# Attention stage: query and key loads of 8 KB rows, 8 in place of 12, three units ahead

## The chip, the cores and the metric

The kernel runs on one core of a Trainium2 chip. The time is device microseconds (us) of one execution: lower is better. Beside the plain runs there is one profiled execution, from which all rows come. Its clock is the granted clock of TensorE: 1.00 stands for 2.4 GHz, 0.50 for 1.2 GHz.

## The reference, cut to what matters

A two-layer gated block works on x of shape (8, 256, 512). Four stages follow one another: an attention with a mask, a ternary-weight feed-forward layer, a long convolution, and an fp8 feed-forward layer. The change touches the attention and the projections ahead of it:

```
q = Wq @ layernorm(x) + bq;  k = Wk @ ctx + bk;  v = Wv @ ctx + bv      # (8, 256, 512)
q, k, v -> (8, 16 heads, 16, 512)                                      # channel = 16 * head + d
dot = einsum('bhdt,bhds->bhts', q, k) / 4
dot = mask * dot - (1 - mask) * 1e6;  amap = softmax(dot) * mask
out = einsum('bhts,bhds->bhdt', amap, v);  x = x + tanh(g) * out
```

## The kernel before, in words

The projection stage (`phase_project`) computes q and k in f32 and splits each into three bf16 parts whose sum is the value. They go to HBM tensors `q_parts` and `k_parts` of shape (8 batches, 3 parts, 256 channels, 512 positions).

The attention stage (`phase_attention`) works on 16 units; a unit u is half a batch, that is 8 heads. For a unit, the SBUF tiles `q_stack` and `k_stack` (`Q` and `K` in the code) hold six blocks of 16 partitions each. A block is one bf16 part of the 16 channels of a head, the 8 heads side by side in the free dimension. With `Q_PART = (0, 0, 1, 1, 0, 2)` and `K_PART = (0, 1, 0, 1, 2, 0)` one bf16 matmul over 128 partitions sums the part products that make an f32 product. Rows 96 to 127 hold the masks and the row maxima. Both tiles have four slots; unit u uses slot u % 4.

Per unit:

- TensorE makes 32 tiles of scores for the maxima (`max_tile`, L707), which VectorE reduces (`reduce_tile`, L793), then the same scores transposed (L728), which ScalarE turns into exponentials (L675), then the products with V (L738). The maxima of unit u+2's first half and of unit u+1's second half are made during unit u. The first tile of unit u+2 comes at step k = 4 of 8 and waits for the loads of that unit, `qk_loaded`.
- The maxima are turned (L716), copied to `mrow` (L653) and sent by DMA into `q_stack` (`place_max`, L529). The first scores of a unit wait for it (`m_placed`).
- `gather_den` (L544 to L550) sends the sums of exponentials of unit u-1 to HBM, waits until they are there (`den_out`), and reads them back spread over 128 partitions. VectorE takes their reciprocal (`invert`, L807); in VectorE's order it stands behind the four tiles of step k = 4. Then come `store_inv` (L556), `spread_inv` (L562) and GpSimd's multiplications (L623 to L631).

All DMAs are issued by SyncE, in program order, on one queue. For each unit u the order is: loads of unit u+2 (`load_unit`, 12 of 128 KB and two of mask rows), `gather_den` of u-1, in every second unit V and mask, `store_inv`, `place_max` of u+1, `spread_inv`, one weight load of 768 KB (L524, wait for `w_ternary`). The load of unit u+2 needs the slot of unit u-2, and so waits for `scores_done` of that unit. The stage begins with the loads of units 0 and 1 (`fresh`: the masks go in once the rows are zeroed), the V load, and two weight loads.

Of the kernel before, what the change touches and what calls it, by code (L numbers as in the profile page):

```python
# [11 lines left out]
P = 128  # L12
B = 8
C = 256
L = 512
CT = C // P
LT = L // P
ROWT = B * CT
HEADS, HD = 16, 16
UH = 8  # L20
# [5 lines left out]
Q_PART = (0, 0, 1, 1, 0, 2)  # L26
K_PART = (0, 1, 0, 1, 2, 0)
BLOCKS = len(Q_PART)
MASK_ROW = BLOCKS * HD
MAX_ROW = MASK_ROW + BLOCKS  # L30
EXTRA = BLOCKS + 2


def batch_loads(b, par):
# [3 lines left out]

def slot_loads(b, par):

    return (2 * BLOCKS + 2) * (8 * (b - par) + 16)


class Core:
# [384 lines left out]
def phase_attention(core, ctx, A):  # L429
# [8 lines left out]
    with ExitStack() as free:  # L438
# [6 lines left out]
        Q = sb("q_stack", [P, 4, UH, L], BF16)  # L445
        K = sb("k_stack", [P, 4, UH, L], BF16)
# [32 lines left out]
        HALF = TILES // 2  # L479
        STATS_STEP, DEN_STEP, TURN_STEP = 2, 4, 4  # L480
        TURN_SLOT = EACH * (TURN_STEP + 1)
        LOADS = 16 * (2 * BLOCKS + 2)

        def tiles(k, more, more2):

# [7 lines left out]
        def over_batches(eng, batch):  # L493

            batch(0, 0, True, False)
            with eng.Fori(0, (B - 2) // 2) as i:
                batch(2 * i + 1, 1, False, False)
                batch(2 * i + 2, 0, False, False)
            batch(B - 1, 1, False, True)

        with nc.Block() as block:

            @block.sync
            def _(sp):
                def load_unit(b, slot, h, fresh=False):
                    for blk in range(BLOCKS):
                        for dst, src, part in ((Q, core.q_parts, Q_PART[blk]), (K, core.k_parts, K_PART[blk])):
                            s = src[bass.ds(b, 1), part, h * P:(h + 1) * P, :]
                            sp.dma_start(dst[blk * HD:(blk + 1) * HD, slot],
                                         s.rearrange("a (h d) l -> d (a h) l", d=HD)).then_inc(qk_loaded[slot], 16)  # L510
                    if fresh:
                        sp.wait_ge(zeroed[slot], 2)
                    for dst, src in ((Q, core.mask_q), (K, core.mask_k)):
                        s = src[bass.ds(b, 1)].rearrange("a r l -> r a l").to_broadcast([EXTRA, UH, L])
                        sp.dma_start(dst[MASK_ROW:MASK_ROW + EXTRA, slot], s).then_inc(qk_loaded[slot], 16)

                def load_batch(b, par):
                    sp.dma_start(V[:, par].rearrange("p a h d -> p (a h d)"),
                                 core.v_rows[bass.ds(b, 1)].rearrange("a p n -> p (a n)")).then_inc(v_loaded[par], 16)
                    sp.dma_start(mb[:, par, :], A["mask"][bass.ds(b, 1), 0, :].to_broadcast([P, L]))\  # L520
                        .then_inc(v_loaded[par], 16)

                def load_weights(u, h):
                    sp.dma_start(wc[:, h], A["w3"][bass.ds(u, 1)].rearrange("a p m l -> p (a m) l"))\  # L524
                        .then_inc(wc_loaded[h], 16)

                def place_max(v, slot, h):
                    sp.wait_ge(mrow_ready, v + 1)
                    sp.dma_start(Q[MAX_ROW:MAX_ROW + 2, slot], mrow[:]).then_inc(m_placed[h], 16)  # L529

                load_unit(0, 0, 0, fresh=True)
                load_unit(0, 1, 1, fresh=True)
                load_batch(0, 0)
                load_weights(0, 0)
                load_weights(1, 1)
                sp.wait_ge(zeroed[2], 2)
                sp.wait_ge(zeroed[3], 2)
                place_max(0, 0, 0)

                def gather_den(u, h, b):  # L540

                    sp.wait_ge(u_ready, 2 * u + 2)
                    rows = core.den_rows[h].rearrange("(g two) l -> two g l", two=2)
                    sp.dma_start(rows[0], num[HD:P:32, h, :]).then_inc(den_out[h], 16)  # L544
                    sp.dma_start(rows[1], odd[HD:P:32, h, :]).then_inc(den_out[h], 16)
                    sp.wait_ge(den_out[h], 32 * (b + 1))
                    sp.dma_start(den[:, h, :], core.den_rows[h].rearrange("q (s n) -> (q s) n", n=DW))\
                        .then_inc(den_placed[h], 16)
                    for g in range(4):
                        sp.dma_start(num[32 * g + HD:32 * g + 32, h, :], odd[32 * g:32 * g + HD, h, :])\  # L550
                            .then_inc(num_placed[h], 16)

                def store_inv(u, h):

                    sp.wait_ge(inv_ready, u + 1)
                    sp.dma_start(core.inv_rows[h].rearrange("q (s n) -> (q s) n", n=DW), inv[:, h, :])\  # L556
                        .then_inc(inv_out[h], 16)

                def spread_inv(h, b):

                    sp.wait_ge(inv_out[h], 16 * (b + 1))
                    sp.dma_start(inv_all[:, h, :], core.inv_rows[h].unsqueeze(1).to_broadcast([UH, HD, L]))\  # L562
                        .then_inc(all_placed[h], 16)

                def batch(b, par, first, last):
                    for h in range(2):
                        u = 2 * b + h
                        if not last:
                            if not first:
                                sp.wait_ge(scores_done, 2 * STEPS * (u - 1))  # L570
                            load_unit(b + 1, 2 * (1 - par) + h, h)
                        if not (first and h == 0):
                            gather_den(u - 1, 1 - h, b + h - 1)
                        if h == 1 and not last:
                            if not first:
                                sp.wait_ge(pv_step, 2 * STEPS * b)
                                sp.wait_ge(w_ready, 2 * b)
                            load_batch(b + 1, 1 - par)
                        if not (first and h == 0):
                            store_inv(u - 1, 1 - h)  # L580
                        if h == 0:
                            place_max(u + 1, 2 * par + 1, 1)
                        elif not last:
                            place_max(u + 1, 2 * (1 - par), 0)
                        if not (first and h == 0):
                            spread_inv(1 - h, b + h - 1)
                        if not (first and h == 0) and not (last and h):
                            sp.wait_ge(w_ternary, 3 * u)
                            load_weights(u + 1, 1 - h)
                    if last:  # L590
                        gather_den(u, h, b)
                        store_inv(u, h)
                        spread_inv(h, b)

                over_batches(sp, batch)

            @block.gpsimd
            def _(pool):
# [1230 lines left out]
```

## Time and profile before

| | us |
|---|---|
| median of 3 runs | 1375.86 (1374.11 to 1379.04) |
| profiled execution, its own time | 1371.15 |
| its span | 1369.3 |
| TensorE busy | 1113.3 (81%) |
| VectorE busy | 1033.2 (75%) |
| ScalarE busy | 668.1 (49%) |
| GpSimd busy | 523.4 (38%) |

The span is the time between the first and the last instruction of the profile. The attention stage lies from about 159 us to 645 us. Idle time in a row is followed by what ended it. The DMA share is the mean busy share of the 16 DMA engines; packets that overlap on an engine can carry it over 1.

### The profile page before, as it was taken

The page shows a single profiled execution, that of the slowest core. Times are in us where ns is not written, and L with a number is a line of the kernel's source. Part 1 is how long each engine was busy: PE and PEld are TensorE (multiplying, and loading weights), DVE is VectorE, ACT ScalarE, POOL GpSimd, SP SyncE. Part 2 cuts the span into 40 slices and gives each one's busy share as a digit, 9 for nine tenths or more (in the row PEclk, how much of TensorE's full clock was granted, in tenths as well). Part 3 has the DMA queues.
Part 4 walks back from the last instruction along what each step waited for, and adds up shares of the span by engine and source line. Part 5 has one row for each costly group of instructions (what it writes and reads, how often), then busy time and mean ns, then how long its engine had stood idle before and what let it go on. Part 6 is the DMA issues. An engine that isn't in the chain of part 4 may idle for free. (4 is left out here: it accounts for less than half of the span.)

```text
span 1369.3 us, 16346 instructions
## 1 busy us (share of the span) xinstructions
PE 1113.3 (81%) x4725; PEld 447.5 (33%) x4802; DVE 1033.2 (75%) x1587; ACT 668.1 (49%) x783; POOL 523.4 (38%) x384
## 2 busy tenths in 40 slices
PE   0887279998879987983799998599999999259777
PEld 0443112222222222220344444344444444134232
DVE  5765488887767877751799997388788887767898
ACT  0355308776657766684466665211000000386796
POOL 0466601244332442355011111477888787000021
PEclk9999659999989999997999999799999999579889
DMA  7398797677756776621311110111111111000011
GB/s 266 127 338 319 199 146 83 119 153 108 125 90 124 151 111 115 114 71 58 151 47 46 40 36 16 35 62 62 62 62 50 58 62 46 1 0 0 0 62 62
DMA packets 84274, 129.33 MB, mean 94 GB/s; under 512 B 13544, under 2 KB 53864, under 8 KB 83696
## 3 DMA queue, kind: packets, MB, share of 16 engines
q1 hardware_dynamic: 84224, 128.72, 38.8%
q8 instruction: 24, 0.39, 0.1%
q14 instruction: 26, 0.21, 0.1%
HBM read 104.44 MB, written 21.89 MB: 92 GB/s over the span
## 5 line engine op out<-in xcount | busy, mean ns | idle before, releaser
L793 DVE TENSOR_REDUCE mneg<-ps_m 128x1 f32<-128x512 f32 x512 | 322.2, 683 | 93.8 <-PE ps_m L707 78.3
L1337 PE MATMUL ps_y<-kv,toeplitz_sb 128*128 128x512 f32 x640 | 279.6, 596 | 8.7 <-POOL kv L1249 8.7
L675 ACT ACTIVATE probs<-ps_s 128x1024 f32<-128x1024 f32 x256 | 249.9, 1022 | 51.9 <-PE ps_s L728 51.9
L707 PE MATMUL ps_m<-k_stack,q_stack 128*128 128x512 bf16 x489 | 181.9, 410 | 55.3 <-DMA k_stack<-mask_k 50.4
L1337 PEld LDWEIGHTS ps_y<-kv,toeplitz_sb 128*128 128x128 f32 x640 | 121.1, 191 | 155.0 <-issue 155.0
L728 PE MATMUL ps_s<-q_stack,k_stack 128*128 128x512 bf16 x492 | 151.0, 387 | 21.1 <-ACT probs L675 11.2
L738 PE MATMUL ps_o<-probs,v_all 128*17 128x512 f32 x1024 | 140.1, 620 | 0.4 <-ACT probs L675 0.4
L1249 POOL TENSOR_TENSOR kv<-vT,ctxT_sb 128x2048 f32<-128x2048 f32 x32 | 118.7, 3711 | 40.0 <-PE ps_y L1337 32.6
L972 PE MATMUL ps_g<-w,xT_f 128*128 128x512 bf16 x491 | 116.7, 384 | 8.4 <-DVE h_f L1119 6.6
L623 POOL TENSOR_TENSOR inv_all<-inv_all,mb_b 128x512 f32<-128x512 f32 x16 | 20.4, 1274 | 254.9 <-DMA inv_all<-inv_rows 254.9
L707 PEld LDWEIGHTS ps_m<-k_stack,q_stack 128*128 128x128 bf16 x512 | 42.2, 99 | 219.4 <-DVE mneg L793 104.5
L1403 DVE TENSOR_TENSOR z<-ps_y,ctxT_sb 128x1024 f32<-128x1024 f32 x64 | 77.9, 1218 | 47.3 <-PE ps_y L1337 47.3
L1302 ACT ACTIVATE w_anchor<-w_f 128x512 f32<-128x512 f32 x32 | 20.1, 628 | 180.6 <-DMA w_f<-in_w 180.6
L1154 POOL TENSOR_TENSOR X<-X,down_sums 128x512 f32 (+1 forms) x16 | 20.5, 1283 | 195.6 <-ACT down_sums L1015 195.6
L1660 PE MATMUL ps_fp<-w 128*128 128x512 bf16 x251 | 67.7, 423 | 21.5 <-DVE w L1727 10.9
L1411 DVE TENSOR_REDUCE vT<-z 128x256 f32<-128x2304 f32 x32 | 81.7, 2553 | 1.1
L54 DVE BATCH_NORM_STATS2 bn<-X (+1 forms) x64 | 42.3, 682 | 42.8 <-POOL X L631 21.2
L728 PEld LDWEIGHTS ps_s<-q_stack,k_stack 128*128 128x128 bf16 x512 | 45.8, 98 | 81.0 <-ACT probs L675 33.9
L641 POOL TENSOR_SCALAR w<-w_sweep 128x512 bf16<-128x512 f32 x48 | 70.4, 1488 | 1.3
L1027 ACT ACTIVATE sg_f<-ps_g,sc_f 128x512 f32<-128x512 f32 x64 | 42.7, 686 | 57.0 <-PE ps_g L972 37.7
L972 PEld LDWEIGHTS ps_g<-w,xT_f 128*128 128x128 bf16 x512 | 48.4, 99 | 65.1 <-DVE h_f L1119 10.3
L326 PE MATMUL ps_a<-xn_a,w_qkv 128*128 128x512 f32 x64 | 30.6, 622 | 38.4 <-DVE xn_a L365 38.4
(163 smaller groups left out, 1662.6 us busy)
## 6 DMA issues: line engine op xcount, KB each, us to landing
w_sweep<-in_w SPq DMA_DIRECT2D x8, 1536.0 KB, 8.5
q_stack<-q_parts SPq DMA_DIRECT2D x96, 128.0 KB
k_stack<-k_parts SPq DMA_DIRECT2D x96, 128.0 KB
w_sweep<-in_w SPq DMA_DIRECT2D x16, 768.0 KB, 6.5
w_sweep<-in_w SPq DMA_DIRECT2D x16, 512.0 KB, 3.3
toeplitz_sb<-in_toeplitz SPq DMA_DIRECT2D x32, 256.0 KB, 2.6
w_f<-in_w SPq DMA_DIRECT2D x32, 256.0 KB, 2.9
q_parts<-qk_part SPq DMA_DIRECT2D x24, 256.0 KB, 4.0
```

The source lines that it names most:

```text
L641: nc.gpsimd.tensor_scalar(core.w3[:, m].rearrange("p a b -> p (a b)")[:, u * L:(u + 1) * L], wc[:, h, m, :], MAGIC, None, ALU.subtract).th ...
L675: nc.scalar.activation(pr[:, k % 2, 2 * slot:2 * slot + 2, :], S[:, 2 * slot:2 * slot + 2, :], ACT.Exp).then_inc(exp_done, 1)
L707: nc.tensor.matmul(M[:, bank(j), :], Q[:, slot, hd, tc * P:(tc + 1) * P], K[:, slot, hd, :], start=True, stop=True).then_inc(max_mm, 1)
L728: mm = nc.tensor.matmul(S[:, g, :], K[:, slot4, hd, (k % LT) * P:(k % LT + 1) * P], Q[:, slot4, hd, :], start=True, stop=True)
L738: mm = nc.tensor.matmul(O[32 * g:32 * g + HD + 1, :], V[:, par, sc, h * UH + 2 * g + G, :], pr[:, k % 2, g, :], start=(sc == 0), stop=(sc ...
L793: nc.vector.tensor_reduce(mneg[:, h, tile % LT, tile // LT:tile // LT + 1], M[:, bank(j), :], AX.X, ALU.max, negate=True).then_inc(max_red, 1)
L972: mm = nc.tensor.matmul(G[:, c % 2, j, :], xT[:, par, k, :], wt[:, k, c * L:(c + 1) * L], start=(k == 0), stop=(k == LT - 1))
L1249: nc.gpsimd.tensor_tensor(kv[:, g % 2].rearrange("p l (b j i) -> p (l b) j i", b=B, j=GROUP), over_j(group(vT, g)), over_i(group(cT, g)), ...
L1337: mm = nc.tensor.matmul(Y[:, q % 3, l2, :], T[:, g % 2, (lt - m) * P:(lt - m + 1) * P], kv[:, g % 2, m, :], start=(m == 0), stop=(m == lt))
L1403: nc.vector.tensor_tensor(z[:, g % 2, NB // 2 * half:NB // 2 * (half + 1), :, 0:GROUP], Y[:, q % 3].rearrange("p l (b j i) -> p (l b) j i" ...
L1411: nc.vector.tensor_reduce(group(vT, g), z[:, g % 2], AX.X, ALU.add).then_inc(red_ready, 1)
L1660: mm = nc.tensor.matmul(D[:, r, :], h8[:, j % 4, L * t + r * P:L * t + (r + 1) * P], proj[:, ot, :], start=(i == 0 and t == 0), stop=(i == ...
```

## The change

Four things change together.

1. The columns of Wq and Wk and the biases are permuted on the host (`by_dim`), in each group of 128 channels from (head, d) to (d, head). In `q_parts` and `k_parts` the 8 heads of one d then follow one another: a row of a block is one piece of 8 x 512 x 2 = 8192 bytes, where it was 8 pieces of 1024 bytes.
2. A unit is loaded by 8 DMAs and not 12. Four of them fill 32 partitions (256 KB): for q, the same part twice (a source with a step of 0 over 2 outside the 16 rows); for k, parts 0 and 1 (a source with 2 parts outside the 16 rows). Four fill 16 partitions (128 KB). The destination and the bytes are as before. `LOADS` follows with 10 in place of 14.
3. The loads of unit u+3, not u+2, are issued in unit u. They wait for `scores_done` of unit u-1. Unit 2's loads come ahead of the loop, and before the weight loads.
4. SyncE's program is written out over all batches, in place of a loop.

The core of the diff:

```diff
-    return (2 * BLOCKS + 2) * (8 * (b - par) + 16)
+    return QK_LOADS * (8 * (b - par) + 16)
...
-                    for blk in range(BLOCKS):
-                        for dst, src, part in ((Q, core.q_parts, Q_PART[blk]), (K, core.k_parts, K_PART[blk])):
-                            s = src[bass.ds(b, 1), part, h * P:(h + 1) * P, :]
-                            sp.dma_start(dst[blk * HD:(blk + 1) * HD, slot],
-                                         s.rearrange("a (h d) l -> d (a h) l", d=HD)).then_inc(qk_loaded[slot], 16)
+                    for dst, src, row, part, times in ((Q, core.q_parts, 0, 0, 2), (K, core.k_parts, 0, None, 1),
+                                                       (Q, core.q_parts, 2, 1, 2), (K, core.k_parts, 2, None, 1),
+                                                       (Q, core.q_parts, 4, 0, 1), (K, core.k_parts, 4, 2, 1),
+                                                       (Q, core.q_parts, 5, 2, 1), (K, core.k_parts, 5, 0, 1)):
+                        if part is None:
+                            s = src[b, 0:2, h * P:(h + 1) * P, :].rearrange("j (d h) l -> j d (h l)", d=HD)
+                            rows = 2
+                        else:
+                            s = src[b, part, h * P:(h + 1) * P, :].rearrange("(d h) l -> d (h l)", d=HD)
+                            s = s.unsqueeze(0).to_broadcast([times, HD, UH * L])
+                            rows = times
+                        sp.dma_start(dst[row * HD:(row + rows) * HD, slot].rearrange("p h l -> p (h l)"), s)\
+                            .then_inc(qk_loaded[slot], 16)
...
                 load_batch(0, 0)
+                load_unit(1, 2, 0, fresh=True)
                 load_weights(0, 0)
                 load_weights(1, 1)
-                sp.wait_ge(zeroed[2], 2)
-                sp.wait_ge(zeroed[3], 2)
                 place_max(0, 0, 0)
...
-                        if not last:
-                            if not first:
-                                sp.wait_ge(scores_done, 2 * STEPS * (u - 1))
-                            load_unit(b + 1, 2 * (1 - par) + h, h)
+                        if u + 3 < 2 * B:
+                            if u:
+                                sp.wait_ge(scores_done, 2 * STEPS * u)
+                            load_unit((u + 3) // 2, (u + 3) % 4, 1 - h, fresh=u == 0)
...
+        return np.ascontiguousarray(v.reshape(v.shape[:-1] + (CT, P // HD, HD)).swapaxes(-1, -2).reshape(v.shape))
...
-        "wqT": np.ascontiguousarray(inputs["L0_xattn_Wq"].T), "wkT": np.ascontiguousarray(inputs["L0_xattn_Wk"].T),
+        "wqT": by_dim(inputs["L0_xattn_Wq"].T), "wkT": by_dim(inputs["L0_xattn_Wk"].T),
```

On SyncE, the end of what is issued ahead of the loop, in the kernel before. L509 is one of the twelve loads of unit 1, L515 the masks, L518 and L520 V and its mask, L524 the weights, L529 the maxima of unit 0.

```order
L509 DMA k_stack<-k_parts 16x8x512
L515 DMA q_stack<-mask_q 8x8x512 [waits zeroed1]
L515 DMA k_stack<-mask_k 8x8x512
L518 DMA v_all<-v_rows 128x1088
L520 DMA mb_b<-in_mask 128x512
L524 DMA w_sweep<-in_w 128x1536 x2
L529 DMA q_stack<-mrow 2x8x512 [waits mrow_ready,zeroed3,zeroed2]
```

The same place now (L527 is V, L518 the loads of unit 2, L524 its masks, L533 the weights, L538 the maxima):

```order
L527 DMA v_all<-v_rows 128x1088
L529 DMA mb_b<-in_mask 128x512
L518 DMA q_stack<-q_parts 32x1x4096
L518 DMA k_stack<-k_parts 32x1x4096
...
L518 DMA q_stack<-q_parts 16x4096
L518 DMA k_stack<-k_parts 16x4096
L524 DMA q_stack<-mask_q 8x8x512 [waits zeroed2]
L524 DMA k_stack<-mask_k 8x8x512
L533 DMA w_sweep<-in_w 128x1536 x2
L538 DMA q_stack<-mrow 2x8x512 [waits mrow_ready]
```

Unit 2's ten DMAs, which stood behind the maxima of unit 0, now stand ahead of them.

On SyncE, unit 1 of the loop in the kernel before, from the last load to the weights:

```order
L509 DMA k_stack<-k_parts 16x8x512
L515 DMA q_stack<-mask_q 8x8x512
L515 DMA k_stack<-mask_k 8x8x512
L544 DMA den_rows<-num 4x512 [waits u_ready]
L545 DMA den_rows<-odd_heads 4x512
L547 DMA den<-den_rows 128x32 [waits den_out0]
L550 DMA num<-odd_heads 16x512 x4
L518 DMA v_all<-v_rows 128x1088
L520 DMA mb_b<-in_mask 128x512
L556 DMA inv_rows<-inv 128x32 [waits inv_ready]
L529 DMA q_stack<-mrow 2x8x512 [waits mrow_ready]
```

The same unit now, where the loads are those of unit 4:

```order
L518 DMA q_stack<-q_parts 32x1x4096 [waits scores_done]
L518 DMA k_stack<-k_parts 32x1x4096
...
L524 DMA q_stack<-mask_q 8x8x512
L524 DMA k_stack<-mask_k 8x8x512
L552 DMA den_rows<-num 4x512 [waits u_ready]
L553 DMA den_rows<-odd_heads 4x512
L555 DMA den<-den_rows 128x32 [waits den_out0]
L558 DMA num<-odd_heads 16x512 x4
L527 DMA v_all<-v_rows 128x1088
L529 DMA mb_b<-in_mask 128x512
L564 DMA inv_rows<-inv 128x32 [waits inv_ready]
L538 DMA q_stack<-mrow 2x8x512 [waits mrow_ready]
```

The order within a unit is the same: the sums of exponentials still go out behind the unit's loads. What moved is that the first load has a wait for `scores_done`, here of unit 0, and that it fills 32 partitions. The orders of the other engines are unchanged.

## Rows read from the trace of the kernel before

**Rows 1.** Waits from 140 to 600 us: total us, times, longest.

```profile
PE ps_m L707 <- DMA k_stack<-mask_k: 50.4, 11, 22.2
...
PE ps_s L728 <- DMA k_stack<-mask_k: 8.0, 3, 3.6
```

**Rows 2.** Timeline, ScalarE: copies that end a unit (start us, us).

```profile
230.57 0.60 ACT L664 ACTIVATE odd_heads<-ps_o 128x512 f32<-128x512 f32 x1 [0.85 <-PE ps_o L738]
...
254.42 0.60 ACT L664 ACTIVATE odd_heads<-ps_o 128x512 f32<-128x512 f32 x1 [0.85 <-PE ps_o L738]
...
305.44 0.60 ACT L664 ACTIVATE odd_heads<-ps_o 128x512 f32<-128x512 f32 x1 [0.77 <-PE ps_o L738]
...
336.02 0.60 ACT L664 ACTIVATE odd_heads<-ps_o 128x512 f32<-128x512 f32 x1 [0.86 <-PE ps_o L738]
...
561.71 0.60 ACT L664 ACTIVATE odd_heads<-ps_o 128x512 f32<-128x512 f32 x1 [0.85 <-PE ps_o L738]
```

**Rows 3.** Timeline, SyncE's issues, one unit of the loop.

```profile
301.65 0.33 SPq L509 DMA_DIRECT2D q_stack<-q_parts  x1
...
309.27 0.50 SPq L545 DMA_DIRECT2D den_rows<-odd_heads  x1
320.06 0.36 SPq L547 DMA_DIRECT2D den<-den_rows  x1
...
327.13 0.70 SPq L529 DMA_DIRECT2D q_stack<-mrow  x1
...
330.16 0.34 SPq L509 DMA_DIRECT2D q_stack<-q_parts  x1
```

**Rows 4.** SyncE's own waits, whole span.

```profile
SPq L547 <- DMA den_rows<-odd_heads: 138.9, 16, 12.4
```

**Rows 5.** Busy time by stretch: per engine; clock, DMA share, GB/s.

```profile
311.00:313.00 2.00, 1.95 (x14) 0.70 (x8) 1.67 (x4) 1.82 (x3) 2.00 (x2) 1.00 1.13 136
...
317.00:319.00 2.00, 0.00 (x0) 0.00 (x0) 0.00 (x0) 0.00 (x0) 0.00 (x0) 0.79 0.37 55
...
321.00:323.00 2.00, 2.00 (x10) 0.16 (x8) 0.85 (x2) 0.00 (x0) 0.00 (x0) 0.50 0.21 44
```

**Rows 6.** Busy time by stretch: V, maxima, reciprocals, ctxT, each alone.

```profile
579.50:581.00 1.50, 1.50 (x11) 0.25 (x10) 1.10 (x2) 1.50 (x3) 0.00 (x0) 1.00 1.00 395
605.00:605.50 0.50, 0.50 (x6) 0.13 (x8) 0.00 (x0) 0.50 (x2) 0.00 (x0) 1.00 0.11 33
...
639.50:640.00 0.50, 0.00 (x0) 0.00 (x0) 0.00 (x0) 0.00 (x0) 0.00 (x0) 0.50 0.51 197
648.00:656.00 8.00, 4.02 (x13) 1.57 (x14) 3.01 (x10) 0.60 (x1) 0.00 (x0) 0.50 1.01 425
```

**Rows 7.** Timeline, SyncE, last unit, nothing else on the queue.

```profile
631.09 0.50 SPq L545 DMA_DIRECT2D den_rows<-odd_heads  x1
632.78 0.32 SPq L547 DMA_DIRECT2D den<-den_rows  x1
```

**Rows 8.** VectorE's reciprocals, the whole run: min, median, max ns.

```profile
L807 DVE RECIPROCAL inv<-den x16: 341/344/353, 244.0 to 634.4; 128x32 f32<-128x32 f32 x16
```

**Rows 9.** Timeline, VectorE, step 4 of unit 5.

```profile
325.33 0.34 DVE L807 RECIPROCAL inv<-den 128x32 f32<-128x32 f32 x1
```

**Rows 10.** Timeline, TensorE: last scores of unit 4.

```profile
300.76 0.59 PE L728 MATMUL ps_s<-q_stack,k_stack 128*128 128x512 bf16 x2
```

**Rows 11.** Timeline, SyncE: first load; maxima of unit 0.

```profile
158.97 0.36 SPq L509 DMA_DIRECT2D q_stack<-q_parts  x1
...
199.14 0.81 SPq L529 DMA_DIRECT2D q_stack<-mrow  x1
```

**Rows 12.** Timeline, TensorE: first maxima, first scores.

```profile
176.38 1.06 PE L707 MATMUL ps_m<-k_stack,q_stack 128*128 128x512 bf16 x2 [22.20 <-DMA k_stack<-mask_k]
...
204.75 0.59 PE L728 MATMUL ps_s<-q_stack,k_stack 128*128 128x512 bf16 x2
```

**Rows 13.** Timeline, VectorE: last statistics of the attention stage.

```profile
645.08 0.69 DVE L54 BATCH_NORM_STATS2 bn<-X 128x6 f32<-128x512 f32 x1 [9.81 <-POOL X L631]
```

More of the change, by code:

```diff
@@ L31 @@
 EXTRA = BLOCKS + 2
+QK_LOADS = 10
 def batch_loads(b, par):
@@ L481, in phase_attention @@
         TURN_SLOT = EACH * (TURN_STEP + 1)
-        LOADS = 16 * (2 * BLOCKS + 2)
+        LOADS = 16 * QK_LOADS
         def tiles(k, more, more2):
@@ L513, in load_unit @@
                     for dst, src in ((Q, core.mask_q), (K, core.mask_k)):
-                        s = src[bass.ds(b, 1)].rearrange("a r l -> r a l").to_broadcast([EXTRA, UH, L])
+                        s = src[b].unsqueeze(1).to_broadcast([EXTRA, UH, L])
                         sp.dma_start(dst[MASK_ROW:MASK_ROW + EXTRA, slot], s).then_inc(qk_loaded[slot], 16)
@@ L593, in batch @@
                         spread_inv(h, b)
-                over_batches(sp, batch)
+                for b in range(B):
+                    batch(b, b % 2, b == 0, b == B - 1)
             @block.gpsimd
@@ L1803, in chunks, with by_dim @@
         return np.ascontiguousarray(np.stack(w, axis=2).transpose(1, 0, 2, 3))
+    def by_dim(v):
+        return np.ascontiguousarray(v.reshape(v.shape[:-1] + (CT, P // HD, HD)).swapaxes(-1, -2).reshape(v.shape))
     eye = np.eye(P, dtype=np.float32)
@@ L1810 @@
         "x": arr("x"), "ctx": arr("ctx_2048"), "mask": arr("mask_Bx1x2048_fk1"), "g_xattn": arr("g_xattn"),
-        "g_ffn": arr("g_ffn"), "bq": columns(inputs["L0_xattn_bq"]), "bk": columns(inputs["L0_xattn_bk"]),
+        "g_ffn": arr("g_ffn"), "bq": columns(by_dim(inputs["L0_xattn_bq"])), "bk": columns(by_dim(inputs["L0_xattn_bk"])),
         "mask_cols": np.ascontiguousarray(inputs["mask_Bx1x2048_fk1"].reshape(B, LT, P).transpose(2, 0, 1)),
         "bv": arr("L0_xattn_bv"),
-        "wqT": np.ascontiguousarray(inputs["L0_xattn_Wq"].T), "wkT": np.ascontiguousarray(inputs["L0_xattn_Wk"].T),
+        "wqT": by_dim(inputs["L0_xattn_Wq"].T), "wkT": by_dim(inputs["L0_xattn_Wk"].T),
         "wvT": np.ascontiguousarray(inputs["L0_xattn_Wv"].T),
```

## The prediction

> **What bounds the kernel now.** I read the waits of the attention stage first, since the change touches nothing later. TensorE waited there 50.4 us and 8.0 us for a unit's loads [rows 1]. 22.2 us of it is the first load; thirteen more waits, the longest of some 4 to 5 us, stand in the middle of units. The marks of unit ends (the copy of the odd heads) show what this costs: 23.85 us between the first two marks, where no wait stood, and 30.58 us in unit 5, which had one of the longest. From the first mark to the thirteenth it is 331.1 us, or 27.6 us a unit [rows 2]. So TensorE's own work allows about 24 us, and the waits, with the clock that falls behind them (0.50, that is 1.2 GHz, after 4 us without work), take 3.6 us a unit [rows 2, 5].
>
> Next I read who sets the time of a load: SyncE. In one unit it began the loads at 301.65, had issued the sums of exponentials by about 309.8, and then stood until 320.06, since these small stores are in the same queue behind the loads: 18.4 us from the first load to their arrival. From there to the next load it took 10.1 us [rows 3]. Over the run this wait is 138.9 us in 16 units [rows 4]. So there is a second loop of about 28 us, through the queue, beside TensorE's 24. What a unit's load costs the queue is the question on which everything else rests.
>
> **What a load costs now.** While the 1 KB pieces go into 16 partitions, all engines are busy (share 1.13) and move only 136 GB/s; at the end, when the mask rows go into 8 partitions, it is 55 GB/s [rows 5]. V's load into 128 partitions moves 395 GB/s at a share of 1.00, and ctxT, in rows of 8 KB, 425 GB/s at 1.01. From the last, an engine moves 425 / 16 = 26.6 GB/s, or 8 KB in 0.31 us.
>
> Two more rows of the same table matter. The reciprocals' spread (L562) reads from a source whose outermost dimension is 8. It moves 197 GB/s at a share of 0.51. The maxima (L529) go into a destination whose outermost dimension is 2. They move 33 GB/s at a share of 0.11 [rows 6]. Eight of 16 engines is 0.50, and two of 16 is 0.125. The transfer is spread over as many engines as its outermost dimension has parts, on whichever side has fewer. The Trainium skill, page "DMA: Bandwidth & Descriptors", section on why a DMA increments its semaphore by 16, says the same in general: the number of engines is the largest up to 16 that divides the slowest dimension of both sides, and they are the lowest-numbered ones. By that rule the trace agrees, in the shares just read; that it is always the same two engines, no row here shows.
>
> **The change part by part.**
>
> *The 32-partition loads.* Their destination is 32 rows, but their source is 2 x 16 rows of 8 KB, with the 2 outermost. By the shares above they run on two engines: four DMAs of 16 rows on each, 64 x 0.31 = 19.7 us. Bounds: the rate of one engine could be that of the maxima (33 / 2 = 16.5 GB/s, 1 KB pieces), which gives 31.8 us; if the loads used all engines, at 425 GB/s they would take 2.5 us. I take 19.7, since ctxT has the same row length.
>
> *The 16-partition loads.* One row of 8 KB on each engine, four DMAs: 1.2 us on the two busy engines. The other 14 engines are done long before.
>
> *The masks.* As before, 8 rows of 8 pieces: 16 pieces on each of 8 engines, at 62 ns (1 KB at 16.5 GB/s): 1.0 us.
>
> A unit's load thus keeps two engines for 19.7 + 1.2 + 1.0 = 21.9 us. Before, 301.65 to 320.06 held loads, masks, a weight load in front and the stores, 18.4 us in all.
>
> *Fewer issues.* Ten in place of 14, by 0.43 us: 1.7 us of SyncE's time. It lies beside the transfers, and SyncE waits behind them anyway: nothing. The same holds for the loop that is written out. If the cover were gone (transfers shorter than the issues) it would be worth 1.7 us a unit.
>
> *Three units ahead.* TensorE no longer waits for a unit's load: it has more than a period longer. What is late next is not the load but what stands in the queue behind it: the sums of exponentials of the unit before, then by SyncE's order the reciprocals and the maxima of the next unit.
>
> *The new wait.* The first load waits for the last scores of unit u-1. The maxima of unit u, which SyncE sent before, let TensorE begin unit u in the meantime. So I take a load to start when unit u-1's scores end. Queued behind it: all of SyncE's chain.
>
> **The new period.** From the first load, S: 1.0 us until bytes move, 21.9 us on the two engines, 1.7 us for the small stores behind them (631.09 to 632.78 with nothing else queued) [rows 7]: den_out at S + 24.6. The sums are read back and VectorE starts the reciprocal 1.6 us later (632.78 to 634.4) [rows 7, 8]: S + 26.2. VectorE executes in order, and this stands behind step 4; steps 5 to 7 of the maxima wait for it, and TensorE, with three banks for them, stops too. In unit 5 it took 10.7 us from the reciprocal (325.33) to the mark (336.02) [rows 2, 9]. The last scores of a unit lie 4.1 us ahead of the mark (301.35 against 305.44) [rows 2, 10]. So the next load starts at S + 26.2 + 10.7 - 4.1 = S + 32.8. TensorE has then stood for over ten microseconds, and works at 1.2 GHz at first. A wait of 4.4 us in unit 5 made 30.58 of 23.85, so the clock cost 2.3; I take 2.2. The period becomes 35 us. SyncE's own chain gives the same: S + 24.6 and 10.1 more is 34.7. From TensorE's side alone nothing would be above 24.
>
> **The start.** Before, the first load is issued at 158.97, the first maxima run at 176.38, the row of maxima is sent at 199.14 and scores begin at 204.75 [rows 11, 12]. Now: bytes from 160.0; units 0 and 1 take two engines until 203.8; V and its mask 1.9 (50 KB an engine); unit 2 another 21.9; the two weight loads 3.6; and the row of maxima, itself a two-engine transfer, 0.5. It lands at 232.7, and scores begin 28 us later than before. The maxima themselves are ready by 208, so the queue decides. The first mark, 25.8 us after the first scores before, comes at 260.8 with 2 us for the clock: 30 us late.
>
> **The sum.** Marks 1 to 13: 12 x 35 = 420 us in place of 331.1: +89. The last three units carry no loads; the wait in unit 13 goes: -3, and the stage's end moves from 645.08 [rows 13] by 30 + 89 - 3 = 116 us. The later stages are as before. 1371.15 + 116 = 1487 for a profiled execution; the median lies 4.7 above the profiled time before, so 1492. Main uncertainty: the period is 32 to 38, twelve times 3 either way, so 1456 to 1528.
>
> **Rivals.**
>
> *The loads use all engines (faster).* Nothing in the rows shows a 2 x 16 source, and the instruction could be regrouped into 32 rows. Then the destination decides. Four loads into 16 partitions at 136 GB/s take 3.9 us, four into twice as many at twice the rate 3.9 us, the masks 2.4: 10 us of queue. TensorE's 24 us bound each unit: 12 x 24.3 = 292 in place of 331, -39; -3 at the end, -4 at the start: 1330. It decides from the point where a load's time in the queue is below 13 us. Against it stand both shares of rows 6. The Trainium skill, page "SBUF — State Buffer", section "Door 1: The DMA port swizzle", says that bandwidth depends on the ports that the partitions reach, four for 16 partitions and two for 8, each about 27 GB/s. The rate of the mask rows agrees (55), that of the 16-partition loads is above it (136, where successive DMAs touch different blocks).
>
> *The depth absorbs it.* If the small transfers did not queue behind the loads, only the two engines' throughput would count: 21.9 and some 5 us of weights, reciprocals and maxima, 27 us a unit, about as now. 12 x 27 = 324, with the start late by 30: 1371 - 7 + 30 - 3, so 1396 with the offset. The wait of 138.9 us [rows 4] speaks against it.
>
> *The two engines are slower.* With both busy on long rows, or the chain of waits longer than added here, the period is 39.5: 12 x 4.5 = 54 more, 1546.
>
> **How the numbers follow.** Period 35 on two engines 0.64, slower still 0.14, depth absorbs 0.10, all engines 0.12. The predicted time is 1492. The range 1435 to 1560 leaves out the fast case, the absorbed one and a little of the slow one's far end. No change means within 0.3%, about what a measurement can tell: 0.01. Faster 0.12, slower 0.87.
>
> **What would show it.** In the profile after: marks about 35 us apart; a DMA share near 0.15 to 0.2 with 50 to 60 GB/s for most of a unit; SyncE's wait for den_rows above 15 us a unit; no wait of TensorE for k_stack in the loop, but one of VectorE for den, over 8 us, in each unit; first scores near 233. Shares near 1 during the loads and marks 24 to 25 us apart would prove the main step wrong; marks at 27 with low shares, the step on the queue.

## The result, and the profile after

| | before | after |
|---|---|---|
| median, 4 runs of each on one chip, us | 1376.97 (1374.11 to 1379.04) | 1557.52 (1555.74 to 1559.64) |
| profiled execution, its own time | 1371.15 | 1555.74 |
| its span | 1369.3 | 1553.9 |
| mean granted clock | 0.918 | 0.875 |

The changed kernel takes 1.133 times as long, interval 1.129 to 1.137. That is 65.5 us above the forecast of 1492 and just inside the range of 1435 to 1560.

The page of the changed kernel: busy time, granted clock and DMA share in 40 slices, packets.

```profile
span 1553.9 us, 15950 instructions
...
PE 1122.1 (72%) x4725; PEld 453.8 (29%) x4802; DVE 1030.1 (66%) x1587; ACT 670.4 (43%) x783; POOL 523.8 (34%) x384
...
PEclk9989557888888888888996999997999999959888
DMA  7597331233233232323214111101112111000011
...
DMA packets 60850, 129.32 MB, mean 83 GB/s; under 512 B 11624, under 2 KB 27368, under 8 KB 57200
```

The engines do the same work in a longer span. The packets fell from 84274 to 60850, so the rows did become longer. But from the fifth slice to the twentieth, the attention stage, the DMA share is only 0.1 to 0.3.

The ends of units (ScalarE's copy of the odd heads, now L673): first, second, third and thirteenth mark, against [rows 2].

```profile
277.50 0.60 ACT L673 ACTIVATE odd_heads<-ps_o 128x512 f32<-128x512 f32 x1 [0.85 <-PE ps_o L747]
...
315.70 0.60 ACT L673 ACTIVATE odd_heads<-ps_o 128x512 f32<-128x512 f32 x1 [0.85 <-PE ps_o L747]
...
356.26 0.60 ACT L673 ACTIVATE odd_heads<-ps_o 128x512 f32<-128x512 f32 x1 [0.85 <-PE ps_o L747]
...
749.28 0.60 ACT L673 ACTIVATE odd_heads<-ps_o 128x512 f32<-128x512 f32 x1 [0.85 <-PE ps_o L747]
```

From the first mark to the thirteenth it is 471.8 us, 39.3 a unit, where it was 331.1 and 27.6.

SyncE in one unit of the loop, from its first load to the next unit's first load, against [rows 3]. The second column is how long the issue itself took.

```profile
312.13 0.66 SPq L518 DMA_DIRECT2D q_stack<-q_parts  x1
...
317.54 9.49 SPq L552 DMA_DIRECT2D den_rows<-num  x1
327.07 0.52 SPq L553 DMA_DIRECT2D den_rows<-odd_heads  x1
343.56 0.35 SPq L555 DMA_DIRECT2D den<-den_rows  x1
...
347.08 0.69 SPq L538 DMA_DIRECT2D q_stack<-mrow  x1
...
349.17 0.34 SPq L533 DMA_DIRECT2D w_sweep<-in_w  x1
...
352.12 0.66 SPq L518 DMA_DIRECT2D q_stack<-q_parts  x1
```

From the first load to the return of the sums it was 18.4 us; here it is 31.4, and 30.4 in the mean of the loop (29.3 to 31.6). From there to the next load it is 8.6 (mean 9.0). The two means add up to the period of 39.3, but for rounding.

The same unit by stretch, against [rows 5, 6]: length, busy time per engine, granted clock, DMA share, GB/s.

```profile
314.00:316.00 2.00, 2.00 (x14) 0.49 (x13) 1.67 (x4) 1.15 (x2) 1.13 (x1) 1.00 0.90 344
316.00:318.00 2.00, 1.47 (x7) 0.34 (x5) 1.80 (x3) 2.00 (x3) 1.84 (x3) 1.00 1.08 162
318.00:320.00 2.00, 2.00 (x14) 0.64 (x14) 1.26 (x2) 1.74 (x3) 1.84 (x3) 1.00 0.97 118
320.00:322.00 2.00, 2.00 (x14) 0.44 (x12) 1.92 (x4) 1.92 (x3) 1.84 (x3) 1.00 0.55 71
...
324.00:342.00 18.00, 7.16 (x45) 1.98 (x37) 5.29 (x11) 6.46 (x8) 1.41 (x1) 0.84 0.13 53
342.00:344.00 2.00, 0.00 (x0) 0.00 (x0) 0.00 (x0) 0.00 (x0) 0.00 (x0) 0.50 0.04 15
```

This is the central row of the case: for 18 us the DMA engines are 0.13 busy, which is 2 of 16, and move 53 GB/s, which is 26.5 GB/s an engine. TensorE stands from 331.3 on (its next matmul, at 346.09, comes after a wait of 14.77), and from 342 to 344 its clock is at 0.50, that is 1.2 GHz.

Who waits for that, 140 to 820 us, in the order of the answer:

```profile
DVE inv L816 <- DMA den<-den_rows: 195.5, 14, 18.6
PE ps_m L716 <- DVE mneg L802: 167.4, 27, 15.5
...
PE ps_m L716 <- DMA k_stack<-mask_k: 42.5, 2, 36.9
...
PE ps_s L737 <- DMA q_stack<-mrow: 25.8, 1, 25.8
```

In [rows 1] TensorE waited for loads fourteen times, eleven for maxima and three for scores. Now it does so twice, both at the start, and in the loop VectorE waits at the reciprocal for the sums, about 14 us a unit, with TensorE behind it for the maxima. In the unit shown, VectorE and then TensorE:

```profile
345.13 0.35 DVE L816 RECIPROCAL inv<-den 128x32 f32<-128x32 f32 x1 [15.77 <-DMA den<-den_rows]
```

```profile
346.09 0.61 PE L716 MATMUL ps_m<-k_stack,q_stack 128*128 128x512 bf16 x1 [14.77 <-DVE mneg L802]
```

The start on TensorE (first maxima, those that waited for unit 1's load, first scores), against [rows 12], and VectorE's end of the stage, against [rows 13]:

```profile
192.01 1.60 PE L716 MATMUL ps_m<-k_stack,q_stack 128*128 128x512 bf16 x3 [36.88 <-DMA k_stack<-mask_k]
...
216.13 2.00 PE L716 MATMUL ps_m<-k_stack,q_stack 128*128 128x512 bf16 x4 [5.59 <-DMA k_stack<-mask_k]
...
251.08 1.03 PE L737 MATMUL ps_s<-q_stack,k_stack 128*128 128x512 bf16 x2 [25.79 <-DMA q_stack<-mrow]
```

```profile
828.74 0.69 DVE L55 BATCH_NORM_STATS2 bn<-X 128x6 f32<-128x512 f32 x1 [9.63 <-POOL X L640]
```

The stage ends 183.7 us later (828.74 against 645.08), of 184.6 us that the span grew. It divides into 46.9 to the first mark, 140.6 from there to the thirteenth, and -3.9 behind it (the parts are rounded). So the loss lies in the attention stage, and three quarters of it in its loop.

### The profile page after: what moved, and what is told of

It is laid out like the page before. It is cut to its first block and busy times, and to the rows that moved or that the text cites. A ratio compares the mean times of both kernels' runs of the same rounds, so it can differ in the third digit from the quotient of the medians.

```text
span 1553.9 us, 15950 instructions
## 1 busy us (share of the span) xinstructions
PE 1122.1 (72%) x4725; PEld 453.8 (29%) x4802; DVE 1030.1 (66%) x1587; ACT 670.4 (43%) x783; POOL 523.8 (34%) x384
## 2 busy tenths in 40 slices
DMA packets 60850, 129.32 MB, mean 83 GB/s; under 512 B 11624, under 2 KB 27368, under 8 KB 57200
## 5 line engine op out<-in xcount | busy, mean ns | idle before, releaser
L716 PE MATMUL ps_m<-k_stack,q_stack 128*128 128x512 bf16 x489 | 187.1, 419 | 210.3 <-DVE mneg L802 167.4
L737 PE MATMUL ps_s<-q_stack,k_stack 128*128 128x512 bf16 x492 | 159.9, 407 | 39.4 <-DMA q_stack<-mrow 25.8
L816 DVE RECIPROCAL inv<-den 128x32 f32<-128x32 f32 x16 | 5.6, 352 | 195.5 <-DMA den<-den_rows 195.5
L737 PEld LDWEIGHTS ps_s<-q_stack,k_stack 128*128 128x128 bf16 x512 | 47.9, 102 | 109.9 <-ACT probs L684 32.8
L981 PEld LDWEIGHTS ps_g<-w,xT_f 128*128 128x128 bf16 x512 | 48.9, 100 | 65.5 <-DVE h_f L1128 9.4
L1036 ACT ACTIVATE sg_f<-ps_g,sc_f 128x512 f32<-128x512 f32 x64 | 42.8, 686 | 58.3 <-PE ps_g L981 39.3
```

The lines of the kernel that those rows point to most:

```text
L716: nc.tensor.matmul(M[:, bank(j), :], Q[:, slot, hd, tc * P:(tc + 1) * P], K[:, slot, hd, :], start=True, stop=True).then_inc(max_mm, 1)
L737: mm = nc.tensor.matmul(S[:, g, :], K[:, slot4, hd, (k % LT) * P:(k % LT + 1) * P], Q[:, slot4, hd, :], start=True, stop=True)
L981: mm = nc.tensor.matmul(G[:, c % 2, j, :], xT[:, par, k, :], wt[:, k, c * L:(c + 1) * L], start=(k == 0), stop=(k == LT - 1))
```

## The experiments

Each edit is against the changed kernel unless it says otherwise. Ratios are to the kernel before, run on the same chip beside it. "Load to sums" is the time from a unit's first load to SyncE's read of the sums. Marks are the ends of units; their distance is the mean from the first to the twelfth, where nothing else is said. The aims were to settle whether two engines are the cause, what part the depth has, and why a load takes 30.4 us and not 24.6.

**The same loads on all engines.** The rows of a pair of blocks are laid out in the order (d, copy), so that the outermost dimension is 16 and not 2. The number of loads, their bytes and row lengths, the depth and the order stay as changed; the sum over rows is the same.

```diff
-s = src[b, 0:2, h * P:(h + 1) * P, :].rearrange("j (d h) l -> j d (h l)", d=HD)
+s = src[b, 0:2, h * P:(h + 1) * P, :].rearrange("j (d h) l -> d j (h l)", d=HD)
...
-s = s.unsqueeze(0).to_broadcast([times, HD, UH * L])
+s = s.unsqueeze(1).to_broadcast([HD, 2, UH * L])
```

> The changed kernel (8 loads, 8 KB rows, three units ahead) with one thing else: the 32-partition loads fill their rows in the order (d, copy) and not (copy, d), so that the source's outermost dimension is 16 and not 2. Theory, the number of engines follows the outermost dimension: these loads now run on 16 engines, the share during a load rises from 0.13 to about 1, the loads leave the queue in 8 to 14 us, VectorE's wait for den goes, marks of unit ends lie 24 to 26 us apart, and the time is 1320 to 1350 us. Rival, the long rows or the few large DMAs themselves cost the queue: rows, number, bytes and order are the same, so the time stays at 1540 to 1570 us.

Measured: 1330.37 us (1329.98 to 1331.58), ratio 0.971 [0.966, 0.976]. SyncE's load to sums, the load's stretch, and the first and twelfth mark:

```profile
283.83 0.62 SPq L517 DMA_DIRECT2D q_stack<-q_parts  x1
...
298.20 0.35 SPq L554 DMA_DIRECT2D den<-den_rows  x1
```

```profile
286.00:288.00 2.00, 2.00 (x14) 0.46 (x13) 1.84 (x4) 1.06 (x2) 1.92 (x3) 1.00 1.05 229
```

```profile
240.22 0.60 ACT L672 ACTIVATE odd_heads<-ps_o 128x512 f32<-128x512 f32 x1 [0.85 <-PE ps_o L746]
...
502.72 0.60 ACT L672 ACTIVATE odd_heads<-ps_o 128x512 f32<-128x512 f32 x1 [0.77 <-PE ps_o L746]
```

Load to sums is 14.4 us here (mean 14.8) in place of 30.4, the share is 1.05 in place of 0.13, the rate 229 GB/s in place of 53, and a unit takes 23.9 us. One order of dimensions is worth 227 us by the two medians, and 222 by the two ratios. The two kernels differ in nothing else, so the outermost dimension of 2 is shown to be the cause.

**Twelve loads of 16 partitions, rows of 8 KB.** The layout and depth of the change, with the loads as they were.

```diff
+for blk in range(BLOCKS):
+    for dst, src, part in ((Q, core.q_parts, Q_PART[blk]), (K, core.k_parts, K_PART[blk])):
+        s = src[b, part, h * P:(h + 1) * P, :].rearrange("(d h) l -> d (h l)", d=HD)
+        sp.dma_start(dst[blk * HD:(blk + 1) * HD, slot].rearrange("p h l -> p (h l)"), s)
```

> The changed kernel with 12 loads of 16 partitions in place of 8: same 8 KB rows, same depth of three units, no source with an outermost dimension of 2. Theory, engines by the outermost dimension and 16 partitions limited to the rate seen before (136 GB/s): a load takes about 12 us of the queue as in the kernel before, TensorE no longer waits for it, the chain from the first load to den_out stays at 18 us, and the time is 1340 to 1370 us. Rival, the row length sets the rate (425 GB/s with 8 KB rows): a load takes about 4 us, marks 24 us apart, 1325 us. Second rival, long rows are what costs: above 1500 us.

Measured: 1385.84 us (1383.03 to 1389.38), ratio 1.012 [1.007, 1.018]; load to sums 18.4, marks 26.8 apart (27.1 to the thirteenth). I had expected 1340 to 1370.

```profile
311.00:313.00 2.00, 2.00 (x13) 0.49 (x14) 1.21 (x2) 2.00 (x3) 1.76 (x4) 1.00 1.04 131
```

**Depth alone.** The kernel before, its 1 KB pieces and twelve loads, with the new order three units ahead.

```diff
+s = src[b, part, h * P:(h + 1) * P, :].rearrange("(h d) l -> d h l", d=HD)
+sp.dma_start(dst[blk * HD:(blk + 1) * HD, slot], s)
```

> The depth alone: 12 loads with the 1 KB pieces and the channel order of the kernel before, but issued three units ahead in the changed kernel's order. Theory: the queue holds as much as before, 18 us from the first load to den_out, TensorE's waits for the loads go, and VectorE waits about 4 us at the reciprocal instead: marks 26 to 27 us apart, 1355 to 1370 us. Rival, the depth and the new order are what made the changed kernel slow (the later start of unit 0's row of maxima, the wait for scores_done): above 1450 us.

Measured: 1384.26 us (1382.39 to 1385.36), ratio 1.011 [1.005, 1.016]; first mark 253.89, against 230.57 in [rows 2], marks 26.8 apart (27.1 to the thirteenth), load to sums 18.2.

```profile
DVE inv L808 <- DMA den<-den_rows: 55.5, 14, 18.7
```

```profile
PE ps_s L729 <- DMA q_stack<-mrow: 19.4, 1, 19.4
```

These two runs differ only in the length of a row, and not in time: 1385.8 and 1384.3. The kilobyte pieces of [rows 5] (136 GB/s) were no slower than rows of 8 KB (131 GB/s), so the length of a row does not set the rate of these loads. The depth costs 23 us at the start, where unit 2's load now stands ahead of the first row of maxima, and gives back 0.5 us a unit in the loop (27.1 against 27.6 in [rows 2], both to the thirteenth mark). I had overlooked the first, and expected 1355 to 1370.

**The change's loads, two units ahead.** The order of the kernel before.

```diff
-                load_unit(1, 2, 0, fresh=True)
...
-                            load_unit((u + 3) // 2, (u + 3) % 4, 1 - h, fresh=u == 0)
+                            load_unit(b + 1, 2 * (1 - par) + h, h)
```

> The changed loads (8, four of them from a source with 2 outermost) with the depth and the place of the kernel before: issued two units ahead, unit 2 inside the loop. Theory, the two engines' time is what counts: the period stays 38 to 41 us, now with TensorE waiting for the load at step 4 as well, but scores of unit 0 begin some 25 us earlier: 1520 to 1560 us. Rival, the depth of three and the order are the fault: back to 1376 us or below.

Measured: 1564.05 us (1562.24 to 1564.65), ratio 1.142 [1.136, 1.147]; first mark 267.52, marks 39.6 apart.

```profile
PE ps_m L717 <- DMA k_stack<-mask_k: 233.5, 16, 36.5
```

I had expected 1520 to 1560, with scores some 25 us earlier; the first mark came 10 us earlier. The same period with another wait: TensorE stands for the load itself. So the depth does not make the loss; it only moves the wait from the load to what is queued behind it.

**Interleaved rows, two units ahead**, the two edits together.

> The interleaved loads (8, rows in the order d, copy, on 16 engines) with the depth and place of the kernel before: two units ahead, unit 2 behind the first row of maxima. Theory, what was wrong before was a load's time in the queue, now 13 us instead of 18: the load lands before step 4, marks stay 23.9 us apart, the first scores begin at 204 to 206 us in place of 213.8, and the time is 1318 to 1326 us. Rival, the depth of three carries the gain: waits of 2 us and more for the load return, above 1335 us.

Measured: 1324.84 us (1322.16 to 1327.7), ratio 0.966 [0.963, 0.968]; marks 24.3 apart, first mark 227.23. Wide loads alone give nearly the whole gain; in the first experiment the depth gained 0.4 us a unit and cost 13 us at the start (240.22).

**Interleaved rows, three ahead, unit 2's load behind the first row of maxima.**

```diff
-                load_unit(1, 2, 0, fresh=True)
                 load_weights(0, 0)
                 load_weights(1, 1)
                 place_max(0, 0, 0)
+                load_unit(1, 2, 0, fresh=True)
```

> The interleaved loads, three units ahead, but unit 2's load behind the first row of maxima. Theory: the start is that of the two-ahead kernel (first scores at 204 to 206 us), the period is TensorE's 23.9 us: 1318 to 1326 us, the same as two ahead. Rival, two loads at once behind the first row of maxima (units 2 and 3, 25 us of queue) delay the row of maxima of unit 1: first mark in place, the second 3 us or more late, 1325 to 1335 us.

Measured: 1320.95 us (1319.45 to 1324.36), ratio 0.963 [0.960, 0.966], the fastest version, if only by 3.9 us, 0.3%, with intervals that overlap. First and twelfth mark:

```profile
227.94 0.60 ACT L672 ACTIVATE odd_heads<-ps_o 128x512 f32<-128x512 f32 x1 [0.85 <-PE ps_o L746]
...
490.44 0.60 ACT L672 ACTIVATE odd_heads<-ps_o 128x512 f32<-128x512 f32 x1 [0.77 <-PE ps_o L746]
```

It has the early start of two ahead and the 23.9 us a unit of three ahead.

**Half of the pairs on two engines.** Rows 0 to 31 as in the change, rows 32 to 63 interleaved.

```diff
+s = s.rearrange("j (d h) l -> j d (h l)" if row == 0 else "j (d h) l -> d j (h l)", d=HD)
```

> The changed kernel with rows 0 to 31 loaded as in the change (outermost dimension 2) and rows 32 to 63 interleaved (outermost 16): two of the four 32-partition loads are left on two engines, 9.9 us of packets in place of 19.7. From the first load to den_out it is 14.4 us with none and 30.3 us with four. Theory A, as in the prediction: the two engines work through their packets from the start while the others do the rest, so it takes 16 to 18 us, marks 24 to 25 us apart, about 1340 us. Theory B: the two-engine packets make progress only once the other engines have finished, so their time adds to the rest: 21 to 23 us, marks 28 to 30 us apart, 1390 to 1420 us.

Measured: 1461.26 us (1459.38 to 1461.91), ratio 1.065 [1.061, 1.069]; marks 32.8 apart.

```profile
354.18 0.66 SPq L520 DMA_DIRECT2D q_stack<-q_parts  x1
...
378.04 0.35 SPq L557 DMA_DIRECT2D den<-den_rows  x1
```

Load to sums is 23.7 us in the mean. Taking 512 KB off two engines should save 9.9 us at 53 GB/s; 6.7 were saved. On all engines these bytes take 2.3 us at the 229 GB/s of the first experiment, and if that does not lie beside the rest, 7.6 is left, near what was measured. The time was missed: I had expected 1390 to 1420.

**The loads on ScalarE's queue.** ScalarE issues the loop's loads of units 4 to 15, two after each of the first five steps, so that nothing small stands behind them in their queue.

```diff
+if 1 <= u and u + 3 < 2 * B and k < 5:
+    if k == 0:
+        act.wait_ge(scores_done, 2 * STEPS * u)
+    for d, s, slot in loads_of((u + 3) // 2, (u + 3) % 4, 1 - h)[2 * k:2 * k + 2]:
+        act.dma_start(d, s).then_inc(qk_loaded[slot], 16)
```

> The changed kernel, with the loads of units 4 to 15 issued by ScalarE, on its own queue, two of the ten after each of the first five steps; the same two-engine transfers. Theory, the period of 39 us comes from the small transfers that stand behind the loads in one queue: now den_out arrives within 5 us of its issue, VectorE's waits for den go, and the period is that of the two engines' throughput, 27 to 31 us: 1400 to 1450 us. Rival, the two engines themselves are saturated whoever issues: the small transfers wait as long as before, 1540 to 1570 us.

Measured: 1492.99 us (1491.79 to 1495.39), ratio 1.089 [1.084, 1.093]; marks 34.2 apart in the mean, alternating between about 30.5 and 37.

```profile
DVE inv L838 <- DMA den<-den_rows: 66.3, 14, 18.3
```

```profile
PE ps_s L759 <- DMA q_stack<-mrow: 79.8, 13, 25.6
```

The wait for the sums fell from 195.5 to 66.3 us, and 79.8 us of waiting for the row of maxima came up. That row goes into an outermost dimension of 2 [rows 6], so it wants two engines itself. The place in the queue, with the issuing engine, is worth about 64 us; the two engines keep the rest of the loss. I had expected 1400 to 1450, and so had put too much on the queue.

**Without the four 16-partition loads.** Rows 64 to 95 are zeroed and not loaded, which leaves out two of the six part products.

```diff
-QK_LOADS = 10
+QK_LOADS = 6
...
-                                                       (Q, core.q_parts, 4, 0, 1), (K, core.k_parts, 4, 2, 1),
-                                                       (Q, core.q_parts, 5, 2, 1), (K, core.k_parts, 5, 0, 1)):
```

> The changed kernel without the four 16-partition loads of a unit: rows 64 to 95 of both tiles are zero, so the smallest part products are left out of the scores; the rest is as in the changed kernel, four 32-partition loads on two engines. From the first load to den_out it is 30.3 us with them. Theory A, their own share on the two engines is all that they cost (four rows, 1.2 us): 29 us, marks 38 us apart, 1535 to 1550 us. Theory B, while the other 14 engines work on them the two engines stand nearly still (window by window the 53 GB/s of the two engines begins 10 us after the first load): 24 to 26 us, marks 33 to 35 us apart, 1480 to 1505 us.

Measured: 1485.17 us (1483.67 to 1488.58), ratio 1.080 [1.075, 1.086]; marks 34.5 apart.

```profile
295.08 0.66 SPq L516 DMA_DIRECT2D q_stack<-q_parts  x1
...
321.46 0.34 SPq L553 DMA_DIRECT2D den<-den_rows  x1
```

Load to sums is 25.7 us in the mean in place of 30.4. These 512 KB, one row of 8 KB on each engine and DMA, cost the queue 4.7 us and not the 1.2 us of the prediction. The time is as I had expected if the two engines hardly advance while the others work: 1480 to 1505.

**The 16-partition loads first.** The same eight loads in another order.

```diff
+for dst, src, row, part, times in ((Q, core.q_parts, 4, 0, 1), (K, core.k_parts, 4, 2, 1),
+                                   (Q, core.q_parts, 5, 2, 1), (K, core.k_parts, 5, 0, 1),
+                                   (Q, core.q_parts, 0, 0, 2), (K, core.k_parts, 0, None, 1),
+                                   (Q, core.q_parts, 2, 1, 2), (K, core.k_parts, 2, None, 1)):
```

> The changed kernel with the four 16-partition loads ahead of the four 32-partition ones. Theory A, each engine works through its own list whatever the others do: the same bytes on the two engines, 30 us from the first load to den_out, 1550 to 1565 us. Theory B, the two engines are slowed only while the others move data at the same time: the 16-partition loads come first for all, about 5 us, and then the two engines run alone at 53 GB/s for 20 us: the sum is 29 to 31 us as well, but the rows differ, the 53 GB/s stretch follows a stretch with 110 to 140 GB/s that contains no 32-partition packets. If the mixture itself wastes time (both slow each other beyond sharing), it falls to 26 to 28 us and 1500 to 1530 us.

Measured: 1540.57 us (1536.3 to 1544.96), ratio 1.119 [1.113, 1.125]; marks 38.5 apart, load to sums 29.3 in the mean.

```profile
310.46 0.34 SPq L518 DMA_DIRECT2D q_stack<-q_parts  x1
...
341.05 0.35 SPq L555 DMA_DIRECT2D den<-den_rows  x1
```

```profile
314.00:316.00 2.00, 1.63 (x11) 0.41 (x5) 1.67 (x3) 1.41 (x3) 1.88 (x2) 1.00 1.17 183
316.00:318.00 2.00, 1.84 (x12) 0.45 (x13) 1.38 (x3) 2.00 (x4) 1.84 (x3) 1.00 0.68 82
...
320.00:322.00 2.00, 2.00 (x14) 0.60 (x7) 1.67 (x4) 1.82 (x3) 2.00 (x3) 1.00 0.13 53
```

The order gains only 1.1 us a unit, and the time lies between the two ranges that I had given (1550 to 1565, 1500 to 1530). Whether the narrow loads stand behind the wide ones or ahead of them, the two kinds take their times nearly one after the other.

## Why the prediction was right or wrong

**Direction and main mechanism: right.** The 32-partition loads run on two engines. The predicted 19.7 us for them is what the trace has for the two engines by themselves: 1 MB at the 53 GB/s of the stretch from 324 to 342 is 19.8 us. The first experiment turns it off with one order of dimensions. The rule of the Trainium skill that I weighed ("DMA: Bandwidth & Descriptors", the section on why a DMA increments its semaphore by 16) held for this source as for the destination and the source of [rows 6]: 0.13 is 2 of 16. That the engines are the same two for every such transfer fits the ScalarE run, where the row of maxima came late, but no row names them.

**Who waits: right.** TensorE does not wait for a load in the loop; VectorE waits at the reciprocal. From the reciprocal to the mark it took 11.1 us (345.13 to 356.26) where 10.7 was forecast.

**The step that failed: a unit's time in the queue.** It was put at 21.9 us, with the sums back at S + 24.6; they came at S + 30.4. The prediction let the two engines run at their full rate from the first microsecond, and the other 14 do their part beside them. That overlap does not exist. Of the 5.8 us, 3.5 are the 16-partition loads: the prediction gave them 1.2 us, their share of the two busy engines; left out, they saved 4.7. The rows show how: from 314 to 322 the engines are 0.55 to 1.08 busy and the rate falls from 344 to 71 GB/s, and only then the two engines begin their 18 us at 53 GB/s, nearly all of their 1 MB. Before that they are not idle but slow. From 318 to 320 the share is 0.97 at 118 GB/s, which is 7.6 GB/s for a busy engine, against 26.5 from 324 on. In the packets of the trace, which name no engine, the same 8 KB take 0.91 to 1.23 us from 318 to 320, and 0.31 from 324 on (median). In the run with loads of 16 partitions only they take 1.00 us from 311 to 313 (median).

The other 2.3 us are still there without these loads (25.7 against 24.6 - 1.2 = 23.4). The weight load, for which the sum had no term, goes with a part of them. In every second unit SyncE issues it close ahead of the first load (311.64 and 312.13), in the others about 3 us ahead (349.17 and 352.12): load to sums is 31.1 us in the former and 29.7 in the latter, and 26.5 and 24.9 without the 16-partition loads. That is 1.5 us in every second unit, or some 0.7 in the mean. No run moves the weight load by itself, and the remaining 1.5 us stay open.

**The rest of the period.** From the sums to the next load it was 9.0 us in the mean, and 10.4 had been taken as the sum of the later steps, with the clock. So the period came out 39.3 and not 35: 5.8 more, 1.4 less, but for rounding. It is the size that the rival of slower engines had (39.5), but not by its cause: the two engines' rate on long rows, by themselves, was as forecast. Twelve periods make 51.6 of the 67.7 us that the stage's end lay beyond the forecast. The time fell inside the range because the range had room for that rival, not because the sum held; that is luck.

**The start.** First scores came at 251.08 and not 232.7, 18.4 us late, by the same step: three unit loads stand ahead of the row of maxima. It is not three times the loop's 5.8, though. TensorE had unit 0's load at 192.01, where the sum had 181.9, and unit 1's at 216.13, where it had 203.8: 10.1 and 12.3 us late. The other 6.1 came with V, unit 2 and the weights. The first mark lay 16.9 us beyond the forecast, the tail -0.9: 51.6 + 16.9 - 0.9 = 67.6, or 67.7 unrounded.

**Slips in the working.** The forecast of the first mark, 260.8, is 260.5 by its own terms (232.7 + 25.8 + 2). The 55 GB/s of the mask rows [rows 5] is the mean of a stretch in which the engines were 0.37 busy, and so not the rate of these transfers; neither the 2.4 us nor the agreement with the ports that were read from it are shown. Neither slip bears on the result.

**Fewer issues, valued at nothing.** As far as the runs show this was right, though none changes the number alone. But the issues became longer: the small store took 9.49 us to issue, where the prediction had 0.43 for an issue. It lies beside the transfers, which bound the unit anyway.

**The rivals.** The one in which the loads use all engines gave 1330 and marks 24.3 apart; built, it took 1330.4, with 23.9. Its condition was not met, and that its price agrees is in part luck. The first mark came 9.6 us later than in [rows 2], not 4 earlier, and twelve units gave 44.7 us, not 39; the span shrank by 39.6 us where 46 were forecast, and the kernel before ran at 1367 beside this run and not at 1376. That the depth absorbs the load is refuted: with the loads in a queue of their own it is still 1493, and with the load two ahead still 1564.

**Left open.** Why packets, those of the two engines among them, take three times as long while the 16-partition loads run. The packets themselves are slow, so the order in which the queue hands out work does not explain it alone. A limit that both share on the writing side, or one at the source, would fit; no run separates them.

## What to carry to other kernels

Read a DMA's outermost dimension on both sides before its size and row length: 16 outside kept all engines at work here, and the same bytes with 2 outside ran at 53 GB/s, 227 us of the kernel. A DMA share that stands at a plain fraction for microseconds (0.13 for 18 us here) is the sign of it. Before loads are issued earlier, ask what small transfer stands behind them on the queue, and in what order the first ones leave.

## What the runs showed of the hardware

- A queue can hold up the engine that issues. With the two engines behind, SyncE's issue of a store took 9.49 us, and at the start these three took 2.1 to 4.7 us:

```profile
165.03 2.10 SPq L524 DMA_DIRECT2D k_stack<-mask_k  x1
167.18 4.72 SPq L518 DMA_DIRECT2D q_stack<-q_parts  x1
171.94 4.55 SPq L518 DMA_DIRECT2D k_stack<-k_parts  x1
```

- At a DMA share near 1 the rate rose with the number of partitions that a load fills: 131 to 136 GB/s into 16, 229 GB/s in the stretch shown where loads fill 32 (205 in the next 2 us), with [rows 6] at 395 into 128. Pieces of 1 KB or of 8 KB made no difference into 16. The size of one DMA grows along with the partitions, and no run separates the two.
- Transfers on two engines and transfers on sixteen hardly overlapped: four loads of 128 KB cost 4.7 us there, where 1.2 us of each engine's time was the estimate. A DMA share near 1 does not mean full speed: 118 GB/s at 0.97 from 318 to 320, with packets of 8 KB at 0.91 to 1.23 us, against 0.31 on two engines alone.
